# Another channel order, other scratch rows and another prologue for the Q/K stacks of an attention and expert layer

## The reference, cut to what matters

```
xn = layernorm(x)
# attention 1: energy = (q1.k1 * scale - threshold) / tau, causal; attn = 1 - tanh(energy)^2, normalized
s  = attention1(xn) @ Wo.T
# block 2
h  = rmsnorm(xn) * norm1_w
X  = xn + softmax(q2.k2 * scale) @ v2 @ wo
h2 = rmsnorm(X) * norm2_w
y  = X + swiglu(h2, shared) + sum_e combine[e] * swiglu(h2, expert_e)
x  = x + s * silu(y)
```

## Time and profile before

| | |
|---|---|
| three runs | 1155.88, 1150.44, 1150.48 us (median 1150.48) |
| the profiled execution | 1157.05 us, span 1155.2 us |
| PE, DVE, ACT, POOL busy | 89%, 74%, 57%, 30% of the span |
| DMA moved | 69.65 MB in 71785 packets, 63056 of them (with smaller ones) under 2 KB |
| first score matmul of row 0 | 76.41 us |
| first score matmul of row 1, of row 2 | 212.24 us, 347.27 us |

### The profile page before, as it was taken

One profiled execution on the slowest core, in us unless ns is written; L12 is line 12 of the kernel. 1 busy time (PEld: TensorE's weight loads), 2 busy tenths in 40 slices (PEclk: granted clock), 3 DMA queues, 4 the chain that ended last, 5 costly groups with the idle time before them and its releaser, 6 DMA issues.

```text
span 1155.2 us, 18598 instructions
## 1 busy us (share of the span) xinstructions
PE 1032.3 (89%) x6912; PEld 471.8 (41%) x6912; DVE 856.3 (74%) x1716; ACT 652.9 (57%) x888; POOL 347.4 (30%) x194
## 2 busy tenths in 40 slices
PE   3459999989999999999999899999999889999998
PEld 1102355324652346423554245522465235542364
DVE  7447687759977597786877589775986869774872
ACT  4027862588326972378624884269723786248831
POOL 6500335103630154303352035400552033520023
PEclk9558999999999999999999999999999999999999
DMA  5540225103441045201251024310342113500020
GB/s 176 117 54 2 49 68 132 34 2 77 109 68 29 3 96 127 38 20 44 64 141 25 11 63 122 69 28 2 96 116 41 30 29 69 148 9 20 1 75 9
DMA packets 71785, 69.65 MB, mean 60 GB/s; under 512 B 8528, under 2 KB 63056, under 8 KB 71568
## 3 DMA queue, kind: packets, MB, share of 16 engines
q1 hardware_dynamic: 68928, 64.41, 24.7%
q10 hardware_dynamic: 2768, 4.06, 1.0%
HBM read 53.37 MB, written 14.81 MB: 59 GB/s over the span
## 4 chain that ended last, share of the span: by engine, by line
PE 56%; DVE 21%; ACT 11%; DMA 4%; issue 3%; SPq 3%; POOL 1%; ACTq 0%; DVEq 0%; POOLq 0%
PE O L1019 9%; PE O L1035 8%; DVE nmax L677 7%; DVE PT L714 7%; ACT PT L554 6%; PE S L1051 6%; PE S L1053 5%; PE S L994 5%; PE S L1052 5%; PE M L963 4%; PE M L960 4%; PE M L946 2%; DVE PT L840 2%; SPq L337 2%; SPq L327 1%
## 5 line engine op out<-in xcount | busy, mean ns | idle before, releaser
L554 ACT ACTIVATE PT<-S 128x1024 f32<-128x1024 f32 (+1 forms) x448 | 420.7, 971 | 117.3 <-PE S L994 115.0
L677 DVE TENSOR_REDUCE nmax<-M 128x1 f32<-128x512 f32 x512 | 330.6, 685 | 119.4 <-PE M L960 80.4
L714 DVE SCALAR_TENSOR_TENSOR PT<-PT 128x768 f32<-128x768 f32 (+1 forms) x192 | 215.6, 1171 | 96.4 <-ACT PT L554 96.0
L1019 PE MATMUL O<-PT,V 128*12 128x256 f32 (+3 forms) x2816 | 242.2, 424 | 0.0
L423 POOL TENSOR_TENSOR split<-split,parts 128x512 f32<-128x512 f32 x32 | 91.0, 2844 | 433.2 <-ACT parts L514 433.2
L438 POOL TENSOR_TENSOR PT<-PT,CB 128x1024 f32<-128x1024 f32 x56 | 133.2, 2385 | 278.0 <-DMA CB<-scrC 158.2
L588 ACT ACTIVATE PT<-S 128x1024 f32<-128x1024 f32 x72 | 73.9, 1027 | 250.7 <-PE S L1053 250.6
L994 PE MATMUL S<-stackQ,stackK 64*128 64x512 bf16 (+3 forms) x1024 | 192.1, 347 | 21.6 <-DMA stackQ<-mTZ 8.4
L1051 PE MATMUL S<-h2hi,wgu_hi 128*128 128x512 f32 x288 | 150.5, 522 | 0.1
L1035 PE MATMUL O<-PT,wdn 128*128 128x512 f32 x288 | 142.7, 595 | 0.0
L960 PE MATMUL M<-KX,stackQ 128*128 128x512 bf16 x256 | 104.3, 409 | 28.5 <-DMA KX<-scrK 21.3
(11 more groups left out here) (189 smaller groups left out, 1042.5 us busy)
## 6 DMA issues: line engine op xcount, KB each, us to landing
CB<-scrC SPq DMA_DIRECT2D x64, 256.0 KB, 5.7
stackQ<-scrQ SPq DMA_DIRECT2D x192, 64.0 KB
stackK<-scrK SPq DMA_DIRECT2D x192, 64.0 KB
scrQ<-parts SPq DMA_DIRECT2D x16, 384.0 KB, 5.0
scrK<-parts SPq DMA_DIRECT2D x16, 384.0 KB, 7.8
KX<-scrK SPq DMA_DIRECT2D x96, 32.0 KB
PT<-in_w_gu ACTq DMA_DIRECT2D x2, 1152.0 KB, 8.0
xin<-in_x SPq DMA_DIRECT2D x8, 256.0 KB, 2.9
```

The lines of the kernel that those rows point to most:

```text
L554: a.activation(PT[:, n % SLOTS, 2 * q * w:2 * q * w + 2 * w].rearrange("p (r n) -> p r n", r=2), S[k][:, :].rearrange("p (r n) -> p r n", ...
L677: v.tensor_reduce(nmax[:, h % 2, h // 2, t:t + 1], M[k][:, :], AX.X, ALU.max, negate=True).then_inc(m_read[k], 1)
L714: v.scalar_tensor_tensor(p, p, 1.0, p, ALU.subtract, ALU.mult).then_inc(weighed, 1)
L1019: last = t_.matmul(O[k][32 * q:32 * q + VW, i0:i1], V[:, j, 4 * g + q, :], PT[:, n % SLOTS, w * q + at:w * q + at + i1 - i0], start=(j == ...
```

## The change

The channels of Q and K (columns of the weights, given by the host) are ordered half, channel, head, where they were head pair, half, channel. In that order the rows of a stack are, for each pair, 64 adjacent partitions of a part. So the scratch in DRAM holds the stack's own rows, `[half, pair, 64, 512]`: each part is stored once for every pair that uses it, by two DMAs (one for each half), six DMAs and 768 KB a stack, in place of one DMA and 384 KB. A stack is then loaded by two DMAs of 48 partitions, each 8 KB in one piece, and KX likewise. `PAIRS` is put in another order so that the copies of a part are evenly spaced (`COPIES`).

In the prologue, ht comes ahead of xn (the same swap is made in the rows), DVE makes the second and third parts of Q2 and K2, and each part is stored when it is there; `KX` is not loaded, and the 32 maxima use the 48-partition form; V1 stands ahead of the maxima, W's maxima stand in one piece behind X's, and `maxT_W` stands behind the first scores. Q1 and K1 are split by POOL behind `wgu_lo`, stored behind the rows of W, and loaded in row 0 behind the rows of Z. The constants that `stack["Q1"]` needs are made by DVE in row 0, after its maxima (`constants`). Waits on `h_ready` by SP become waits on `xn_ready`, the last of the two.

```diff
-PAIRS = [(0, 0), (0, 1), (0, 2), (1, 0), (1, 1), (2, 0)]
+PAIRS = [(0, 2), (0, 0), (0, 1), (1, 0), (1, 1), (2, 0)]
+COPIES = {"Q": (slice(0, 3), slice(3, 5), slice(5, 6)), "K": (slice(1, 6, 2), slice(2, 5, 2), slice(0, 1))}
...
-PLACES[16] += ["xnT", "hT"]
+PLACES[16] += ["hT", "xnT"]
...
+START = PLACES | {16: ["hT"], 18: ["K2", "xnT"], UNITS - 1: PLACES[UNITS - 1] + ["V1"],
+                  EXPERT + 4: [w for w in PLACES[EXPERT + 4] if w != "V1"],
+                  EXPERT + 5: [w for w in PLACES[EXPERT + 5] if w not in MAX["W"]],
+                  EXPERT + 6: MAX["W"][:1] + ["maxT_X"] + MAX["W"][1:], EXPERT + 7: [], EXPERT + 8: []}
...
-FIRST = Uses(False, True)
+FIRST = Uses(False, True, places=START)
...
+STORED = 3 * 2 * 16
...
-        scratch = {n: nc.dram_tensor("scr" + n, [3, 128, L], bf16).ap() for n in stack}
+        scratch = {n: nc.dram_tensor("scr" + n, [2, len(PAIRS), HALF, L], bf16).ap() for n in stack}
...
+        def store_part(engine, name, i, part):
+
+            at = COPIES[name[0]][part]
+            copies = len(range(*at.indices(len(PAIRS))))
+            for r in range(2):
+                engine.dma_start(scratch[name][r, at].rearrange("c p n -> p c n"),
+                                 parts[i % 2][HALF * r:HALF * r + HALF, part:part + 1, :].broadcast_to([HALF, copies, L]))\
+                    .then_inc(stored[name], 16)
+
+        def load_stack(engine, name, bt):
+
+            engine.wait_ge(stored[name], (bt + 1) * STORED)
+            if name == "K2" and (not isinstance(bt, int) or bt > 0):
+                for r in range(2):
+                    engine.dma_start(KX[HALF * r:HALF * r + ROW_ADD, r, :, :],
+                                     scratch[name][r].rearrange("c (d h) n -> (c d) h n", h=HP)[:, 0:PADDED, :]).then_inc(stacked_KX, 16)
+            for r in range(2):
+                engine.dma_start(stack[name][HALF * r:HALF * r + ROW_ADD, :, :],
+                                 scratch[name][r].rearrange("c (d h) n -> (c d) h n", h=HP)).then_inc(stacked[name], 16)
...
-            def restack(names, first, bt):
-
-                for i, name in enumerate(names):
-                    sp.wait_ge(parts_ready, bt * 4 + first + i + 1)
-                    sp.dma_start(scratch[name].rearrange("a p n -> p a n"), parts[(first + i) % 2][:, :, :]).then_inc(stored[name], 16)
...
+            def restack(name, i, bt):
+
+                sp.wait_ge(parts_ready, bt * 4 + i + 1)
+                for part in range(3):
+                    store_part(sp, name, i, part)
+                load_stack(sp, name, bt)
...
-                    restack(("Q2", "K2"), 0, bt)
-                    sp.wait_ge(setup, 2)
-                    restack(("Q1", "K1"), 2, bt)
+                    for i, name in enumerate(("Q2", "K2")):
+                        for part, (ready, value) in enumerate((read(u, name), (second_part, i + 1), (parts_ready, i + 1))):
+                            wait_apart(sp, ready, value)
+                            store_part(sp, name, i, part)
+                    for name in ("Q2", "K2"):
+                        load_stack(sp, name, bt)
...
+                if it is None:
+                    for i, name in ((2, "Q1"), (3, "K1")):
+                        sp.wait_ge(parts_ready, i + 1)
+                        for part in range(3):
+                            store_part(sp, name, i, part)
...
+                if it == 0:
+                    sp.wait_ge(setup, 2)
+                    for name in ("Q1", "K1"):
+                        load_stack(sp, name, 0)
...
-                act.wait_ge(tau_step, 3)
-                a.activation(pt[3][:, :], pt[2][:, :], ACT.Ln).then_inc(tau_step, 1)
...
                     if name == "V2":
+                        act.wait_ge(tau_step, 3)
+                        a.activation(pt[3][:, :], pt[2][:, :], ACT.Ln).then_inc(tau_step, 1)
                         act.wait_ge(gu_in, 32)
...
+                if n == 0:
+                    take(FIRST, "maxT_W", 0)
...
+                    if it == 0 and n == 10:
+                        constants()
...
+            for i, name in enumerate(("Q2", "K2")):
+                s, p = split[i], parts[i]
+                dve.wait_ge(*read(FIRST, name))
+                step(v.tensor_tensor(s[:, :], s[:, :], p[:, 0, :], ALU.subtract))
+                v.tensor_copy(p[:, 1, :], s[:, :]).then_inc(second_part, 1)
+                dve.wait_ge(second_part, i + 1)
+                v.tensor_tensor(p[:, 2, :], s[:, :], p[:, 1, :], ALU.subtract).then_inc(parts_ready, 1)
...
-                if name in MAX["X"] or name in MAX["W"]:
+                if u is not FIRST and (name in MAX["X"] or name in MAX["W"]):
...
+        channels = np.arange(D).reshape(HP, 2, HD).transpose(1, 2, 0).reshape(D)
```

More of the change, by code:

```diff
@@ L470, in _ @@
                                 ALU.subtract).then_inc(pv_done, SLOTS // 2)
+            for name in ("Q1", "K1"):
+                for _step in split_steps(FIRST, name, 0, False):
+                    pass
             for it in range(B):
@@ L615, in _ @@
                         act.wait_ge(setup, 1)
[L616 removed]
+                    if name != "maxT_W":
+                        take(FIRST, name, 0)
                     if name == "V2":
+                        act.wait_ge(tau_step, 3)
+                        a.activation(pt[3][:, :], pt[2][:, :], ACT.Ln).then_inc(tau_step, 1)
                         act.wait_ge(gu_in, 32)
@@ L1203, in _ @@
                 for name in FIRST.places[n]:
-                    work(FIRST, -1, name)
+                    if name != "maxT_W":
+                        work(FIRST, -1, name)
             pe.wait_ge(dn_in, 16)
@@ L1207, in _ @@
             first_scores(0)
+            work(FIRST, -1, "maxT_W")
             for q in range(2):
```

111 lines of the change are left out of this document (50 added, 61 removed).

## The result

The changed kernel takes 1145.32 us (median of 16 executions, 1143.36 to 1150.04), the kernel before 1153.64 (16 executions, 1148.97 to 1160.69). The ratio is 0.9929, with a 95% interval from 0.9913 to 0.9946: faster by 0.7%. I had forecast 1127.9, with a range from 1121.5 to 1136. The sign is right and the size is not: 8.3 us in place of 22.6. The profiled execution of the changed kernel took 1145.48 us (span 1143.7). In the runs further down two single executions, of 1867 and 3996 us, were slow and are left out of every median and ratio.

A forecast was written before the change was run, and what follows sets the result against it. The prediction took the prologue as bound by the restack (SP's issues, slow loads) and rows by PE. Gain 23.2 - 0.3 - 0.3 = 22.6 us, subtracted from the median 1150.48, gave 1127.9 us; range 1121.5 to 1136.

The forecast's parts named there:

- the third row of X: Prologue: 14.71 us of DMA wait behind this row's load, ending at 76.17 just ahead of the first scores, would go.
- the new loads would fill the engines: Restack: loads of 48 partitions run on 16 DMA engines, those of 8 partitions on 8; DMA share well over 0.6.
- the maxima take 22.2 us: Prologue: 22.9 us without the gap for V1, less 0.7 for PE's last maximum, from 31.0 to first scores at 53.2.
- The stores: Prologue: twelve DMAs at 0.38 us of issue each, the last out at 21.6 and landed 3.5 us later, at 25.1.
- Q2's falls behind its own stores and is over before K2's: Prologue: Q2's stack load does not delay K2's, which is issued at 25.9 and lands at about 31.
- the rivals' sum: Slow-load estimate, x for two stacks: K2 lands at 22 + 1.7 + x, Q1/K1 at 35.2 + 1.7 + x; gain zero at 18.7.
- The price of a stack: Stack loads: half the weights' rate, about 210 GB/s, so 3.7 us a stack, plus 1.7 us to land.
- a part of the gain only: Rival: loads at 100 to 180 GB/s or stores landing late, 1131 to 1145 us, middle 1137; chance 0.17.
- K1 may be late by up to 1 us. I take 0.3.: Row 0: Q1 and K1 loaded by 44.4 us after first scores, stage 2 starting at 44.05; loss between 0 and 1.
- the rival of slow loads: Loads keep the old rate, delaying both prologue and row 0: 1161.6 us at 65 GB/s, 1137.7 at 128; slower: chance 0.04.
- The prologue is not what differs as far as the profile can say, so I subtract from the median.: Whole kernel: the gain is taken from the median 1150.48 us, not from the profiled execution of 1157.05.
- its case of no change: Rival: gain eaten by row 0, two stacks loading in near 18 us, 1150 us, within 0.5%; chance 0.04.

The follow-up runs named there:

- memsets_later: Changed kernel, but POOL's last two memsets (stack of K1 and KX) wait for xn, and SP waits for them later: 1144.35 us, ratio 0.9919.
- the runs of loads: Two kernels that only make DMAs and compute nothing of the reference; half a stack took 4.2 us (4.7 a second time), both halves 6.4.
- order_only: Changed kernel with the old layout, each part stored once and twelve loads of eight partitions a stack: 1154.13 us, ratio 1.0019.
- after_again: Changed kernel run once more without edit, for a second profile: 1146.75 us, ratio 0.9926.

## Why the prediction was wrong, step by step

**What held.** That the prologue alone would change, and the rows not. That the third row of X was the end of the chain and would go. That the new loads would fill the engines. That the maxima take 22.2 us from first to first scores: 22.1 (38.48 to 60.60). The stores were costed wrongly on both sides: 0.67 us of issue each and not 0.38, but K2's load follows the last of them after 1.5 us (26.31 to 27.77) and not 4.3; without the delay by the memsets it is issued at 25.25 (`memsets_later`), forecast 25.9. That the two errors nearly cancel is luck.

**"Q2's falls behind its own stores and is over before K2's"** is the step that failed first. In the queue as printed ahead of the prediction both loads stand behind all twelve stores. Q2's is issued at 26.35, not at the 22 that the rivals' sum takes for it, and it is on its way until 33.38, 5.6 us after K2's issue at 27.77. K2's lands 10.0 us after its issue, and 5.4 were forecast (3.7 for the stack, 1.7 to land). The miss at the first maximum is 7.5 us (38.48 for 31.0): K2's load issued 1.9 late, 4.6 more from issue to landing, 0.7 from the landing over PE to DVE, which no term held, and 0.3 of rounding. In the terms of the rivals' sum (22 + 1.7 + x) it is 4.4 for the place in the queue (with the delay told below in it) and 2.2 for the price of two stacks, 11.4 us in place of 9.2.

**The price of a stack** was my own guess, half of the rate of the weights. The halves land 2.1 to 2.3 us apart, at about 180 GB/s and not 210; that rate is the upper end of the 100 to 180 GB/s that I had given to the rival "a part of the gain only". And the fixed part taken from a small row, 1.7 us, is too short: one half alone took 4.2 to 4.7 us in the runs of loads.

**A cost that no term held.** The memset of `stack["K1"]`, moved to POOL, keeps DVE's small steps waiting. `root` takes 2.90 us for 1.45, and the step behind it starts 1.76 later than in the kernel before (9.50 for 7.74; 0.31 of this is a later input). It is in the 1.9 us by which K2's load is issued late. I had read the diff for SP, PE, ACT and DVE, and POOL's list not at all.

The maxima themselves took what was forecast, so the first scores stand at 60.60 for 53.2, 7.4 us.

**"K1 may be late by up to 1 us. I take 0.3."** The wait is 3.39 us, with a further 1.56 behind stage 2, where the clock had fallen. Counted from the first scores, the two loads go out from 33.75 (forecast 35.2) and the last lands 11.5 us later (forecast 9.2), so K1 is there at 45.3 (forecast 44.4 at the latest). PE is ready for it at 41.98, not at 44.05. The cover of 44.05 us was read from the one execution of three in which the clock rose late; the other two had 42.2 and 42.3. Row 0 as a whole loses 2.9 us against the profile of before, forecast 0.6: 2.3 us of the miss. Six profiles of four kernels that load Q1 and K1 in the prologue, with the clock up early, have a row 0 of 132.8 to 133.2; against these it loses 4.3 to 4.8. That a late stack costs twice, in the prologue and in row 0, is what the rival of slow loads said (x counted twice); `order_only` shows it with the old loads: 12.0 us.

**"The prologue is not what differs as far as the profile can say, so I subtract from the median."** Three profiles of before do not settle this. The shortest of them (1147.56 us) differs from the first by 5.7 us in the prologue and 1.9 in row 0; the one nearest to the median (1154.36) by 0.1 in the prologue and 1.6 in row 0. What they do show is that the 44.05 us from the first scores to stage 2, from which I took K1's cover, belong to an execution with a late clock. The profiled execution was 3.4 us above the median of 16, the changed kernel's 0.2 above its own: 3.2 us of the miss are between 11.5 in the profiles and 8.3 in the medians. And the median of three, 1150.48, was 3.2 below that of sixteen.

The sum: 7.4 (first scores) + 2.3 (row 0) + 1.4 (single longer rows) + 3.2 (profile against median) is 14.3, which is 22.6 less 8.3; with 3.2 for the base it is the 17.4 us between 1127.9 and 1145.32. By the borders of the prediction 1145.32 lies just inside its case of no change (from 1144.7, chance 0.04), but only because the median of three stood low; against sixteen executions the gain of 0.7% is clear.

**What stays open.** Why 48 partitions take as long as 64, and 96 longer than 128. Why the landing of the rows of X varies by 5 us between executions, and what sets the moment at which the clock rises in row 0. What the fourth memset costs by itself. That POOL's memset and DVE's steps meet at a port was read from their durations, not measured by itself on an empty chip.

## What to carry to other kernels

When a transfer is moved to a later place, its cover is the time until its reader is ready, and that time differs between executions (44.1, 42.3 and 42.2 us here): take the shortest, or the wait comes back in the fast ones. The loads here landed in the order of their issue, so the time of the last is that of all the bytes ahead of it (11.4 us for two stacks, 6.4 to 6.6 for one); and stores put behind a load land behind it too (3.7 to 5.8 us for 2.0 to 2.8), so changing the order of the two stacks gained nothing. Before a gain is subtracted from a median, take more than one profile: the same wait differed here by 5.4 us between executions, and the start of stage 2 by 1.9. And read what POOL does while DVE makes small pieces on the critical path.

## What the runs showed of the hardware

- Four DVE pieces that take 0.17 us by themselves ended together with the POOL instruction beside them: 2.90 us over a memset of 1.80 and the end of the one before, 1.45 over the end of a single one, 4.90 and 4.95 beside POOL's 5.02. Reductions over PSUM are not held (0.69 us each with POOL busy, 0.70 with POOL idle).
- Loads of 8 KB rows from DRAM land in 2.8, 3.0, 4.5, 4.6, 5.4 and 4.8 us for 16, 32, 48, 64, 96 and 128 partitions: from 48 to 128 the bytes grow 2.7 times and the time by 0.3 us. The Trainium skill ("DMA: Bandwidth & Descriptors", section "Anatomy of one DMA — SWDGE (gpsimd) path") has a fit of a fixed 2.0 us and 436 GB/s, made for another kind of issue. An estimate by it is 2.9 us for 48 and 4.4 for 128; the runs show 4.5 and 4.8, so the fit is near for 128 rows and 1.6 us short for 48.
- Loads on one queue landed in the order of issue: four of 384 KB, issued from 26.35 to 28.5, at 31.08, 33.38, 35.69 and 37.77.
- Each wait of PE for K1 was followed by a lower clock, and the time from stage 2 to `warm` grew from the 90.60 of before: after 3.39 us of wait by 1.56 (clock 0.56 over the next 3 us), after 3.33 in `after_again` by 2.09 (0.50), after 3.97 in `memsets_later` by 2.32 (0.50), after 12.02 in `order_only` by 1.76 (0.50). So this cost does not grow with the wait.
